# The cluster means of a fused convolution kernel, taken from the tiles in SBUF

## The chip, the cores and the metric

The kernel runs on one core of one Trainium2 chip. The metric is the device time of one execution in microseconds (us), as a median over several runs. A profiled execution is read beside it; its rows give the busy times, the waits and the order of the work. TensorE is called PE in those rows, its weight loads PEld, VectorE DVE, ScalarE ACT, GpSimd POOL and SyncE SP; a "q" behind an engine means its DMA issues.

## The reference, cut to what matters

The input `x` has 8 batches of 512 channels of 128 x 128. The first layer (L0) halves it with a grouped convolution, finds 8 clusters among the 256 channels of batch 0 alone, and takes the mean of each cluster's channels in every batch. A mixture model is fitted to those means, and what it gives scales the image in the rest of the layer. The second layer (L1) is a filtered resampling with a leaky slope.

```python
x = conv(sx, w_down, strides=(2, 2), padding=1, groups=256)    # (8, 256, 64, 64), 3x3, 2 inputs each
xx = x[0].reshape(256, 4096)                                     # batch 0 alone
labels = _kmeans_labels((xx - mn) / (mx - mn))                   # 10 rounds, 8 clusters
...                                                              # slabel: labels sorted by spread
soh = one_hot(slabel, 8)
v5 = einsum('bchw,ck->bkhw', x, soh / maximum(soh.sum(0), 1))   # the cluster means, all batches
mu, var = _gmm_fit(v5)                                           # 10 rounds, 2 components
...                                                              # gate from mu and var
out = L1(_bilinear_up_x2(up(gate * x + x)) + sx)
```

So the means of all batches need the labels, the labels need the convolution of batch 0 alone, and the mixture needs all means.

## The kernel before, in words

The program is five blocks, one behind another, with a barrier of all engines between them.

`convolution()` (line 133 on) goes through 64 units, 8 for each batch. A unit is 128 of the 256 channels (`cb`, two of them, `CB`) and 16 of the 64 output rows (`q`, four quarters, `NQ`). SP loads a unit's input rows into one of two buffers `rows_in` (line 186, about 4.2 MB), once DVE and PE have done the unit that used the buffer (`v_done`, `t_done`). DVE makes the first 9 of the 16 rows with one TENSOR_SCALAR (line 231) and 17 SCALAR_TENSOR_TENSOR (line 235), each waiting for the one before. PE makes the other 7 with 18 matmuls against diagonal weights (line 256); each fp32 matmul is two instructions in the trace, so a unit is 36. ACT copies PE's 7 rows from PSUM into the unit's tile `conv` (line 275) and stores the whole tile of 128 x 1024 to DRAM, `conv_dram` (line 281). The 8 units of batch 0 are written out; those of batches 1 to 7 are the body of a loop, so there are six jumps back. Within a batch the order is four quarters of `cb` 0, then four of `cb` 1 (`cb, q = n // NQ, n % NQ`). Units with `q == 0` are a little shorter on DVE, for they lack the row above.

`clusters(soh, sohn)` loads batch 0 back from `conv_dram` (`xx`), runs the k-means, and leaves the sorted labels as `soh` and their normalised form as `sohn`, 128 x 2 x 8.

`cluster_means(sohn)` (line 536 on) loads each batch back from `conv_dram` (`xb`, 4 MB, line 558), multiplies it on PE by `sohn` in pieces of 512 columns (line 569: 8 pieces of two channel blocks for each batch, outputs on 8 PSUM partitions), copies each piece on ACT (line 581), and stores the means to `mean_dram` (line 583).

`mixture(soh)` starts by loading `mean_dram` (line 650). `resample()` is the second layer with the end of the first; it reads `conv_dram` and `x` again and writes the output. Neither is touched.

The order on each engine is the order in which the code is written; no scheduler moves anything.

Of the kernel before, what the change touches and what calls it, by code (L numbers as in the profile page):

```python
# [13 lines left out]
P = 128  # L14
# [14 lines left out]
QR = 16  # L29
# [59 lines left out]
def build(nc, x, w_down, w_conv, w_up, bias, up_filter, down_filter, consts, out):  # L89
    at = constants()[1]  # L90
    ctx = ExitStack()
    with ctx:
# [40 lines left out]
        def convolution():  # L133
            with ExitStack() as own:
# [7 lines left out]
                tap_w = sb("tap_w", [P, CB, TAPS])  # L142
                diag = sb("diag", [P, CB * TAPS, P])
# [9 lines left out]
                UB = CB * NQ  # L153

                order = [(i, kh, kw) for i in range(2) for kh in (1, 0, 2) for kw in (1, 0, 2)]

                def conv_in(n, i, kh, kw, r0, r1):

                    c0 = (1, 0, 1)[kw]
                    return rows_in[n % 2][:, i, 2 * r0 + kh:2 * (r1 - 1) + kh + 1:2, c0:c0 + 2 * (63 if kw == 0 else 64) - 1:2]  # L160
# [4 lines left out]
                def _(sp):  # L165
# [11 lines left out]
                    def load(b, n, wait):  # L177
                        cb, q = n // NQ, n % NQ
                        if wait is not None:

                            sp.wait_ge(v_done, wait)
                            sp.wait_ge(t_done, wait)
                        lo = 1 if q == 0 else 0
                        src = x[bass.ds(b, 1)] if not isinstance(b, int) else x[b:b + 1]
                        src = src.rearrange("o (b c i) h w -> (o b) c i h w", b=CB, i=2)[cb]
                        sp.dma_start(rows_in[n % 2][:, :, lo:, :],
                                     src[:, :, 2 * QR * q - 1 + lo:2 * QR * (q + 1), :]).then_inc(in_loaded[n % 2], 16)

                    for n in range(UB):
                        load(0, n, n - 1 if n >= 2 else None)  # L190
                    with sp.Fori(1, B) as b:
                        for n in range(UB):
                            load(b, n, UB * b + n - 1)

                @block.vector
                def _(v):
# [21 lines left out]
                    def unit(b, n, first):  # L218
                        cb, q = n // NQ, n % NQ
                        v.wait_ge(in_loaded[n % 2], 16 * (n // 2 + 1) if first else (16 * (UB // 2)) * b + 16 * (n // 2 + 1))  # L220
                        if not (first and n < 2):

                            v.wait_ge(conv_stored[n % 2], 16 * (n // 2) if first else (16 * (UB // 2)) * b + 16 * (n // 2))
                        for s, (i, kh, kw) in enumerate(order):
# [3 lines left out]
                            src = conv_in(n, i, kh, kw, r0, V_ROWS)  # L228
                            last = s == TAPS - 1
                            if s == 0:  # L230
                                ins = v.tensor_scalar(dst, src, w, None, ALU.mult)
                            else:

                                v.wait_ge(vec_step, (TAPS - 1) * n + s if first else (TAPS - 1) * UB * b + ((TAPS - 1) * n + s))
                                ins = v.scalar_tensor_tensor(out=dst, in0=src, scalar=w, in1=dst, op0=ALU.mult, op1=ALU.add)  # L235
                            ins.then_inc(v_done if last else vec_step, 1)

                    for n in range(UB):
                        unit(0, n, True)
                    with v.Fori(1, B) as b:  # L240
                        for n in range(UB):
                            unit(b, n, False)

                @block.tensor
                def _(pe):
                    pe.wait_ge(diag_ready, 1)

                    def unit(b, n, first):
                        cb = n // NQ
                        pe.wait_ge(in_loaded[n % 2], 16 * (n // 2 + 1) if first else (16 * (UB // 2)) * b + 16 * (n // 2 + 1))  # L250
                        if not (first and n < 2):

                            pe.wait_ge(t_copied, n - 1 if first else UB * b + (n - 1))
                        acc = bank[n % 2][:, 0:T_ROWS * WO].rearrange("p (r w) -> p r w", r=T_ROWS)
                        for s, (i, kh, kw) in enumerate(order):
                            mm = pe.matmul(acc[:, :, (1 if kw == 0 else 0):],  # L256
                                           diag[:, cb * TAPS + (i * 3 + kh) * 3 + kw, :],
                                           conv_in(n, i, kh, kw, V_ROWS, QR), start=(s == 0), stop=(s == TAPS - 1),
                                           skip_group_check=True)
                        mm.then_inc(t_done, 1)  # L260

                    for n in range(UB):
                        unit(0, n, True)
                    with pe.Fori(1, B) as b:
                        for n in range(UB):
                            unit(b, n, False)

                @block.scalar
                def _(act):
                    def unit(b, n, first):  # L270
                        cb, q = n // NQ, n % NQ
                        act.wait_ge(t_done, n + 1 if first else UB * b + (n + 1))
                        if not (first and n < 2):
                            act.wait_ge(conv_stored[n % 2], 16 * (n // 2) if first else (16 * (UB // 2)) * b + 16 * (n // 2))
# [3 lines left out]
                        act.wait_ge(t_copied, n + 1 if first else UB * b + (n + 1))  # L278
                        act.wait_ge(v_done, n + 1 if first else UB * b + (n + 1))
                        rows = conv_dram[cb * P:(cb + 1) * P] if first else conv_dram[bass.ds(C * b + cb * P, P)]  # L280
# [3 lines left out]
                    for n in range(UB):  # L284
                        unit(0, n, True)
# [988 lines left out]
```

## Time and profile before

| | us |
|---|---|
| median of 3 runs (lowest to highest) | 7656.16 (7654.64 to 7658.82) |
| the profiled execution's own time | 7660.9 |
| its span, first to last instruction | 7658.7 |
| convolution, last group of 17 on DVE: begin, length | 1012.05, 14.43 |
| last issue of the convolution's stores | 1026.69 |
| first load of `cluster_means` issued | 1206.51 |
| first load of the mixture issued | 1336.74 |

Over the whole span PE is busy for 7119.1 us (93%), DVE for 5921.4 (77%), ACT for 4596.5 (60%) and POOL for 2518.8 (33%). These shares mix stages with different limits, and the resampling is by far the longest, so for a change in the first 1340 us the stages have to be read one by one. The page's 40 slices are 191 us each: the convolution is the first five and a bit, the clusters, the means and the mixture are the next three.

### The profile page before, as it was taken

What the parts mean: (1) busy time and instruction counts of PE and PEld (TensorE: products, weight loads), DVE (VectorE), ACT (ScalarE), POOL (GpSimd) and SP (SyncE); (2) the same over time, 40 slices, a digit from 0 to 9 for tenths busy, and PEclk for the clock granted to TensorE, in tenths of its full rate; (3) what the DMA queues carried; (4) which work ended last, traced back from release to release, by engine and by line L of the source; (5) the groups of instructions that cost most, each with busy time, mean ns of one, the idle gap of its engine ahead of it and who ended that gap; (6) DMA issues with size and microseconds to landing.
All of it is one profiled execution on the core that took longest, in us unless ns stands there. A gap on an engine that the chain in (4) does not pass through costs nothing.

```text
span 7658.7 us, 691127 instructions
## 1 busy us (share of the span) xinstructions
PE 7119.1 (93%) x302021; PEld 6407.7 (84%) x302021; DVE 5921.4 (77%) x11619; ACT 4596.5 (60%) x9070; POOL 2518.8 (33%) x3076
## 2 busy tenths in 40 slices
PE   7999967029999999999999999999999999999999
PEld 3444442029999999999999999999999999999998
DVE  8999950877777777777777777777777777777776
ACT  0000002337777777777777777777777777777776
POOL 0000000014444444444444444444444444444443
PEclk9999978569999999999999999999999999999999
DMA  7777724003333333333333333333333333333332
GB/s 303 316 310 308 310 118 183 3 24 96 96 96 96 96 96 96 96 96 96 96 96 96 96 96 96 96 96 96 96 96 95 96 96 96 96 96 96 96 96 80
DMA packets 1261531, 925.62 MB, mean 121 GB/s; under 512 B 183504, under 2 KB 1233104, under 8 KB 1242576
## 3 DMA queue, kind: packets, MB, share of 16 engines
q1 hardware_dynamic: 1252112, 890.13, 36.2%
q10 hardware_dynamic: 9344, 34.61, 1.7%
q8 instruction: 32, 0.52, 0.0%
q14 instruction: 43, 0.35, 0.0%
HBM read 621.50 MB, written 303.04 MB: 121 GB/s over the span
## 4 chain that ended last, share of the span: by engine, by line
PE 78%; issue 0%; DVE 0%; DMA 0%; ACT 0%; SPq 0%; POOL 0%; DVEq 0%
PE bank L1009 26%; PE bank L1004 24%; PE twin L1004 13%; PE twin L1009 13%; PE twin L1139 2%; DVE x_sum L1237 0%; DMA img<-in_x 0%; DVE leaky L1213 0%; DMA low<-conv_dram 0%; SPq L915 0%; ACT dn L1204 0%; ACT slope_t L1173 0%; POOL img L963 0%; DVE up L1222 0%; SPq L916 0%
## 5 line engine op out<-in xcount | busy, mean ns | idle before, releaser
L1213 DVE SCALAR_TENSOR_TENSOR leaky<-bank,slope_t 128x512 f32<-128x512 f32 x4096 | 2636.5, 685 | 1034.9 <-ACT slope_t L1173 1034.9
L1004 PE MATMUL bank<-up_t,up 64*64 64x133 f32 x65536 | 2760.3, 276 | 7.1 <-issue 6.3
L1009 PEld LDWEIGHTS bank<-down_t,leaky 64*64 64x64 f32 x131072 | 2235.9, 135 | 101.8 <-issue 92.9
L1009 PE MATMUL bank<-down_t,leaky 64*64 64x35 f32 (+1 forms) x131072 | 2306.3, 222 | 10.0 <-issue 8.0
L1173 ACT ACTIVATE slope_t<-bank 128x512 f32<-128x512 f32 x4096 | 2225.6, 599 | 7.9 <-PE bank L1004 7.9
L1004 PEld LDWEIGHTS bank<-up_t,up 64*64 64x64 f32 x65536 | 2041.1, 133 | 9.5 <-issue 9.5
L972 POOL TENSOR_TENSOR low_d<-low_v 128x252 f32<-128x252 f32 x512 | 310.9, 607 | 5038.9 <-ACT low_v L1195 5038.9
L1189 ACT ACTIVATE res<-twin 128x512 f32<-128x512 f32 x1024 | 611.6, 597 | 1447.7 <-PE twin L1009 1447.7
L1237 DVE SCALAR_TENSOR_TENSOR x_sum<-lift,coef,img 128x128 f32<-128x128 f32 x4096 | 1428.9, 409 | 11.7 <-POOL img L963 11.7
L1004 PE MATMUL twin<-up_t,x_sum 64*64 64x133 f32 x32768 | 1386.5, 278 | 9.2 <-DVE x_sum L1237 5.3
L1009 PE MATMUL twin<-down_t,dn 64*64 64x35 f32 (+1 forms) x65536 | 1358.8, 221 | 6.0 <-issue 5.7
L1009 PEld LDWEIGHTS twin<-down_t,dn 64*64 64x64 f32 x65536 | 1263.6, 135 | 6.8 <-issue 6.8
L1204 ACT ACTIVATE dn<-bank 128x512 f32<-128x512 f32 x2048 | 1135.5, 625 | 8.3 <-PE bank L1009 8.3
L963 POOL TENSOR_TENSOR img<-img,bias_all 128x512 f32<-128x512 f32 x1024 | 1041.7, 1036 | 7.5 <-DMA img<-in_x 7.3
L256 PE MATMUL twin<-rows_in,diag 128*128 128x448 f32 (+1 forms) x2304 | 929.5, 560 | 95.1 <-DMA rows_in<-in_x 91.4
L1004 PEld LDWEIGHTS twin<-up_t,x_sum 64*64 64x64 f32 x32768 | 1008.3, 133 | 10.8 <-issue 10.8
L1222 DVE COPY up<-twin 128x512 f32<-128x512 f32 x1024 | 708.6, 692 | 294.8 <-PE twin L1004 273.7
L256 PEld LDWEIGHTS twin<-rows_in,diag 128*128 128x128 f32 x2304 | 431.1, 189 | 592.8 <-issue 522.0
L235 DVE SCALAR_TENSOR_TENSOR conv<-rows_in,tap_w,conv 128x576 f32<-128x576 f32 (+3 forms) x1088 | 880.9, 810 | 45.3 <-issue 7.0
L1182 ACT ACTIVATE up<-twin 128x512 f32<-128x512 f32 x1024 | 611.6, 597 | 123.0 <-PE twin L1004 76.7
L275 ACT ACTIVATE conv<-twin 128x448 f32<-128x448 f32 x64 | 34.8, 544 | 988.3 <-PE twin L256 988.3
L978 POOL TENSOR_TENSOR lift<-low_f,low_v 128x504 f32<-128x504 f32 x512 | 565.5, 1105 | 40.1
(154 smaller groups left out, 2154.7 us busy)
## 6 DMA issues: line engine op xcount, KB each, us to landing
img<-in_x SPq DMA_DIRECT2D x1024, 256.0 KB, 2.9
out<-res SPq DMA_DIRECT2D x1024, 256.0 KB, 2.2
rows_in<-in_x SPq DMA_DIRECT2D x48, 4224.0 KB, 14.0
rows_in<-in_x SPq DMA_DIRECT2D x16, 4096.0 KB, 13.8
conv_dram<-conv ACTq DMA_DIRECT2D x64, 512.0 KB, 4.2
xb<-conv_dram SPq DMA_DIRECT2D x8, 4096.0 KB, 13.2
low<-conv_dram SPq DMA_DIRECT2D x1024, 32.0 KB, 2.2
xx<-conv_dram SPq DMA_DIRECT2D x2, 2048.0 KB, 10.3
```

Of the source, the lines that this page charges most:

```text
L235: ins = v.scalar_tensor_tensor(out=dst, in0=src, scalar=w, in1=dst, op0=ALU.mult, op1=ALU.add)
L256: mm = pe.matmul(acc[:, :, (1 if kw == 0 else 0):], diag[:, cb * TAPS + (i * 3 + kh) * 3 + kw, :], conv_in(n, i, kh, kw, V_ROWS, QR), star ...
L963: nc.gpsimd.tensor_tensor(pix, pix, bg[:, :, None].to_broadcast([P, 4, W]), ALU.add).then_inc(biased, 1)
L1004: return pe.matmul(acc[cols(c), a:b], src[cols(rt), cols(c)], up_t[cols(rt), a:b], start=first, stop=False, skip_group_check=True)
L1009: return pe.matmul(acc[cols(c), a:b], src[cols(rt)], down_t[cols(rt), k, a:b], start=first, stop=False, skip_group_check=True)
L1173: nc.scalar.activation(slope_t[e][i][:], u2_acc[e][i][:], ACT.Copy, scale=SLOPE * GAIN).then_inc(slope_out, 1)
L1182: nc.scalar.activation(up1[p][:, 0].rearrange("p e h -> p (e h)"), u1_acc[0], ACT.Copy).then_inc(u1_out0, 1)
L1189: nc.scalar.activation(res[1 - p][:].rearrange("p (e i) w -> p e (i w)", e=2), twin[:, :, 0:D2], ACT.Copy).then_inc(res_ready, 1)
L1204: nc.scalar.activation(dn1[p][:, e].rearrange("p j i h -> p (j i h)"), d1_acc[e][:], ACT.Copy).then_inc(d1_out, 1)
L1213: v.scalar_tensor_tensor(out=leaky[1 - m % 2][:, e, i].rearrange("p k w -> p (k w)"), in0=u2_acc[e][i][:], scalar=GAIN, in1=slope_t[e][i][ ...
L1222: v.tensor_copy(up1[m % 2][:, 1].rearrange("p e h -> p (e h)"), u1_acc[1]).then_inc(u1_out1, 1)
L1237: ins = v.scalar_tensor_tensor(out=x_sum[n % 2][:, e, i, :], in0=lift[n // 2][:, 2 * (n % 2) + e, :], scalar=cf, in1=img[n % 2][:, e, i, : ...
```

## The change

The convolution is split in two. `first_convolution()` does the 8 units of batch 0 alone. `clusters()` follows, and now keeps `xx` and the weights beyond its end; the normalised labels are written into `sohp`, 128 x 2 x 32, whose columns 8 to 31 are zero. `other_convolutions(sohp, xx)` then does the 56 units of batches 1 to 7 and makes the means on the way. `cluster_means()` is gone. Within a batch the units alternate between the channel blocks (`cb, q = n % CB, n // CB`), so that the two units of one quarter are neighbours.

A unit's means are four matmuls (line 341 of the changed kernel), for the four quarters of its 1024 columns: 128 x 32 weights, 256 columns each, and each writes 32 PSUM partitions of its own (`acc[32 * c:32 * (c + 1)]`). PE does unit n's taps first and then the means of unit n-1, when DVE's and ACT's parts of that tile are in (`v_done`, `t_copied`). The two units of a quarter add up in one PSUM bank (2 or 3, in turn). ACT copies that bank as 128 x 256 into `cm` and stores it with four DMAs (`store_means`). The tile of unit n-2 may only be written again when its means are made: DVE and ACT wait for `mean_mm` in addition to what they waited for. Batch 0's means are made from `xx` before PE's first taps of batch 1. Batch 1 is written out and batches 2 to 7 are a loop, so there are five jumps back.

Three places, as the engines' instructions stand. PE, in the written-out part, from the end of one unit to the begin of the one after (before: `twin` is the PSUM of the taps, `diag` the weights):

```order
L256 MATMUL twin<-rows_in,diag 128x7x63
L256 MATMUL twin<-rows_in,diag 128x448
L256 MATMUL twin<-rows_in,diag 128x448 [waits t_copied,in_loaded0]
L256 MATMUL twin<-rows_in,diag 128x7x63
L256 MATMUL twin<-rows_in,diag 128x448 x2
```

The same place in the changed kernel:

```order
L361 MATMUL twin<-rows_next,diag 128x7x63
L361 MATMUL twin<-rows_next,diag 128x448
L341 MATMUL bank<-conv_next,sohp 32x256 [waits mean_copied,next_t_copied,next_v_done]
L341 MATMUL bank<-conv_next,sohp 32x256 x3
L361 MATMUL twin<-rows_next,diag 128x448 [waits next_t_copied,next_loaded0]
L361 MATMUL twin<-rows_next,diag 128x7x63
```

Four matmuls have moved in between the last tap of a unit and the first of the next, and they wait for DVE and ACT. DVE, at the first instruction of a unit, before:

```order
L235 SCALAR_TENSOR_TENSOR conv<-rows_in,tap_w,conv 128x9x63 [waits vec_step]
L235 SCALAR_TENSOR_TENSOR conv<-rows_in,tap_w,conv 128x576 [waits vec_step]
L231 TENSOR_SCALAR conv<-rows_in,tap_w 128x576 [waits conv_stored1,in_loaded1]
L235 SCALAR_TENSOR_TENSOR conv<-rows_in,tap_w,conv 128x9x63 [waits vec_step]
L235 SCALAR_TENSOR_TENSOR conv<-rows_in,tap_w,conv 128x576 [waits vec_step] x2
```

and now, in the convolution of the other batches:

```order
L332 SCALAR_TENSOR_TENSOR conv_next<-rows_next,tap_w,conv_next 128x9x63 [waits next_step]
L332 SCALAR_TENSOR_TENSOR conv_next<-rows_next,tap_w,conv_next 128x576 [waits next_step]
L329 TENSOR_SCALAR conv_next<-rows_next,tap_w 128x576 [waits mean_mm,next_stored1,next_loaded1]
L332 SCALAR_TENSOR_TENSOR conv_next<-rows_next,tap_w,conv_next 128x9x63 [waits next_step]
L332 SCALAR_TENSOR_TENSOR conv_next<-rows_next,tap_w,conv_next 128x576 [waits next_step] x2
```

The unit's first instruction has one wait more, for PE. SP, from the clusters' loads to the mixture's, before:

```order
L362 DMA xx<-conv_dram 128x4096 x2
L294 UNCONDITIONAL_BRANCH
L553 UNCONDITIONAL_BRANCH [waits barrier_Pool_Activation_PE_DVE_SP_release]
L558 DMA xb<-conv_dram 128x2x4096 x2
L558 DMA xb<-conv_dram 128x2x4096 [waits cm_mm] x6
L537 UNCONDITIONAL_BRANCH
L647 UNCONDITIONAL_BRANCH [waits barrier_Pool_Activation_PE_DVE_SP_release]
L650 DMA data<-mean_dram 16x8x256 x8
```

and now, up to the first loop:

```order
L490 DMA xx<-conv_dram 128x4096 x2
L422 UNCONDITIONAL_BRANCH
L304 UNCONDITIONAL_BRANCH [waits barrier_Pool_Activation_PE_DVE_SP_release]
L147 DMA rows_next<-in_x 128x2x4096 x2
L147 DMA rows_next<-in_x 128x2x4224 [waits next_t_done,next_v_done] x6
L296 UNCONDITIONAL_BRANCH
```

The eight loads `xb` are gone, and the first loads of batch 1 stand behind the clusters' barrier. Behind the last unit, ACT has one copy of 128 x 256 (line 386) and four stores of means (line 392) ahead of the barrier before the mixture. The diff, cut to its core:

```diff
-        def convolution():
+        def load_rows(sp, rows_in, in_loaded, b, n):
+            cb, q = n % CB, n // CB
...
+        def first_convolution():
...
-                    for n in range(UB):
-                        load(0, n, n - 1 if n >= 2 else None)
-                    with sp.Fori(1, B) as b:
-                        for n in range(UB):
-                            load(b, n, UB * b + n - 1)
+                    for n in range(UB):
+                        if n >= 2:
+                            sp.wait_ge(v_done, n - 1)
+                            sp.wait_ge(t_done, n - 1)
+                        load_rows(sp, rows_in, in_loaded, 0, n)
...
+        def other_convolutions(sohp, xx):
...
+                def cnt(b, n, per=1, of=1):
+                    return (UB // of * per) * b + ((n // of) - UB // of) * per
+                def batches(eng, unit):
+                    for n in range(UB):
+                        unit(1, n)
+                    with eng.Fori(2, B) as b:
+                        for n in range(UB):
+                            unit(b, n)
...
+                @block.vector
+                def _(v):
+                    def unit(b, n):
+                        cb, q = n % CB, n // CB
+                        v.wait_ge(in_loaded[n % 2], cnt(b, n + 2, per=16, of=2))
+                        if ahead(b, n, 2):
+                            v.wait_ge(conv_stored[n % 2], cnt(b, n, per=16, of=2))
+                            v.wait_ge(mean_mm, cnt(b, n + UB - 1))
...
+                @block.tensor
+                def _(pe):
+                    def means(acc, tile, cb):
+                        for c in range(4):
+                            mm = pe.matmul(acc[32 * c:32 * (c + 1), 0:256], sohp[:, cb, :], tile[:, 256 * c:256 * (c + 1)],
+                                           start=(cb == 0), stop=(cb == CB - 1), skip_group_check=True)
+                        mm.then_inc(mean_mm, 1)
+                    def means_of(b, n):
+                        pe.wait_ge(v_done, cnt(b, n + 1))
+                        pe.wait_ge(t_copied, cnt(b, n + 1))
+                        if n % CB == 0:
+                            pe.wait_ge(mean_copied, cnt(b, n, of=2) + (NQ - 1))
+                        means(bank[2 + n // CB % 2], conv[n % 2][:].rearrange("p r w -> p (r w)"), n % CB)
+                    def unit(b, n):
...
+                        mm.then_inc(t_done, 1)
+                        if n > 0:
+                            means_of(b, n - 1)
+                        elif ahead(b, n, 1):
+                            means_of(b - 1, UB - 1)
+                    for g in range(NQ):
+                        if g >= 2:
+                            pe.wait_ge(mean_copied, g - 1)
+                        for cb in range(CB):
+                            means(bank[2 + g % 2], xx[:, cb, QR * WO * g:QR * WO * (g + 1)], cb)
+                    batches(pe, unit)
+                    means_of(B - 1, UB - 1)
...
+                    def store_means(b, q):
+                        act.wait_ge(mean_mm, cnt(b, 2 * q + 2 + UB))
+                        if not (isinstance(b, int) and NQ * b + q < 2):
+                            act.wait_ge(cm_stored[q % 2], cnt(b, 2 * q + UB, per=4 * 16, of=4))
+                        nc.scalar.activation(cm[q % 2][:], bank[2 + q % 2][:, 0:256], ACT.Copy).then_inc(mean_copied, 1)
+                        act.wait_ge(mean_copied, cnt(b, 2 * q + 2 + UB, of=2))
...
+                        for c in range(4):
+                            at = QR * WO * q + 256 * c
+                            act.dma_start(dst[:, at:at + 256], cm[q % 2][32 * c:32 * c + K]).then_inc(cm_stored[q % 2], 16)
...
-        def cluster_means(sohn):
...
-        convolution()
-        clusters(soh, sohn)
-        cluster_means(sohn)
+            first_convolution()
+            xx = own.enter_context(nc.sbuf_tensor("xx", [P, CB, PX], F32))
+            clusters(soh, sohp, xx)
+            other_convolutions(sohp, xx)
```

## Rows read from the trace of the kernel before

**Rows 1.** The page, part 4: chain that ended last, shares by engine.

```profile
PE 78%; issue 0%; DVE 0%; DMA 0%; ACT 0%; SPq 0%; POOL 0%; DVEq 0%
```

**Rows 2.** Windows: length, busy of PE, PEld, DVE, ACT, POOL; clock, DMA, GB/s.

```profile
160.00:1027.00 867.00, 810.92 (x2014) 375.66 (x2012) 811.97 (x1009) 30.47 (x56) 0.00 (x0) 0.99 0.77 307
1027.00:1206.50 179.50, 96.82 (x406) 76.93 (x406) 55.36 (x182) 17.04 (x26) 0.00 (x0) 0.66 0.07 27
1206.50:1336.70 130.20, 112.58 (x256) 23.09 (x256) 0.00 (x0) 37.57 (x64) 0.00 (x0) 0.93 0.68 266
1690.00:7659.00 5969.00, 5942.82 (x298406) 5848.57 (x298405) 4633.09 (x9178) 4395.90 (x8683) 2499.44 (x3049) 1.00 0.33 95
```

**Rows 3.** Timeline of DVE, convolution: start us, length us, instruction, idle before.

```profile
531.71 0.81 DVE L231 TENSOR_SCALAR conv<-rows_in,tap_w 128x576 f32<-128x576 f32 x1 [2.29 <-issue]
...
536.97 10.77 DVE L235 SCALAR_TENSOR_TENSOR conv<-rows_in,tap_w,conv 128x512 f32<-128x512 f32 x13 [1.18 <-issue]
547.65 0.81 DVE L231 TENSOR_SCALAR conv<-rows_in,tap_w 128x576 f32<-128x576 f32 x1
...
562.85 0.80 DVE L231 TENSOR_SCALAR conv<-rows_in,tap_w 128x576 f32<-128x576 f32 x1
...
593.23 0.81 DVE L231 TENSOR_SCALAR conv<-rows_in,tap_w 128x576 f32<-128x576 f32 x1
...
608.01 0.81 DVE L231 TENSOR_SCALAR conv<-rows_in,tap_w 128x576 f32<-128x576 f32 x1
...
656.03 0.81 DVE L231 TENSOR_SCALAR conv<-rows_in,tap_w 128x576 f32<-128x576 f32 x1 [2.38 <-issue]
```

**Rows 4.** Waits, convolution's window: us in total, times, longest.

```profile
DVE conv L231 <- issue: 14.0, 6, 2.4
DVE conv L235 <- issue: 7.0, 6, 1.2
```

**Rows 5.** Timeline of PE, convolution: two units.

```profile
592.49 14.42 PE L256 MATMUL twin<-rows_in,diag 128*128 128x448 f32 x36 [0.39 <-DMA rows_in<-in_x]
607.51 14.43 PE L256 MATMUL twin<-rows_in,diag 128*128 128x448 f32 x36 [0.60 <-DMA rows_in<-in_x]
```

**Rows 6.** Timeline of ACT, convolution: the copies behind those units.

```profile
592.13 0.54 ACT L275 ACTIVATE conv<-twin 128x448 f32<-128x448 f32 x1 [13.54 <-PE twin L256]
...
607.02 0.54 ACT L275 ACTIVATE conv<-twin 128x448 f32<-128x448 f32 x1 [14.35 <-PE twin L256]
```

**Rows 7.** Source L186, the loads of rows_in.

```profile
DMA to landing us min/median/max: 13.4/14.0/33.9
```

**Rows 8.** Timeline of ACT, start of the kernel: the first unit's copy.

```profile
54.71 0.55 ACT L275 ACTIVATE conv<-twin 128x448 f32<-128x448 f32 x1 [52.68 <-PE twin L256]
```

**Rows 9.** Timeline of PE, start of the kernel: the first units.

```profile
37.73 31.10 PE L256 MATMUL twin<-rows_in,diag 128*128 128x448 f32 x72 [37.73 <-DMA rows_in<-in_x]
```

**Rows 10.** Timeline, cluster_means: its first loads.

```profile
1206.51 29.48 SPq L558 DMA_DIRECT2D xb<-conv_dram  x3
```

**Rows 11.** Timeline of PE, cluster_means: from the first landing on.

```profile
1219.31 5.98 PE L569 MATMUL twin<-xb,sohn 128*8 128x512 f32 x8 [13.94 <-DMA xb<-conv_dram]
1225.13 3.60 PE L569 MATMUL bank<-xb,sohn 128*8 128x512 f32 x8
```

**Rows 12.** Timeline, end of cluster_means and start of the mixture.

```profile
1332.57 0.27 ACTq L583 DMA_DIRECT2D mean_dram<-cm  x1
1336.74 3.65 SPq L650 DMA_DIRECT2D data<-mean_dram  x8
```

**Rows 13.** Lines by form, cluster_means: busy us, mean ns, idle before.

```profile
L569 PE MATMUL bank<-xb,sohn 128*8 128x512 f32 x124 | 55.8, 592 | 0.0
...
L569 PEld LDWEIGHTS bank<-xb,sohn 128*8 128x8 f32 x125 | 11.2, 90 | 42.4 <-issue 42.4
```

**Rows 14.** Timeline of PE, resampling: two groups of 64x64 matmuls.

```profile
3001.58 0.66 PE L1004 MATMUL bank<-up_t,up 64*64 64x133 f32 x16
3002.04 0.66 PE L1004 MATMUL twin<-up_t,x_sum 64*64 64x133 f32 x16
```

More of the change, by code:

```diff
@@ L152, in convolution @@
                 t_copied = sem("t_copied")
[L153 to L160, printed above, removed]
                 block = own.enter_context(nc.Block())
@@ L216, in _ @@
                             n += 1
[L218 to L223, printed above, removed]
+                    for n in range(UB):
+                        cb, q = n % CB, n // CB
+                        v.wait_ge(in_loaded[n % 2], 16 * (n // 2 + 1))
+                        if n >= 2:
+                            v.wait_ge(conv_stored[n % 2], 16 * (n // 2))
                         for s, (i, kh, kw) in enumerate(order):
@@ L246, in _ @@
                     pe.wait_ge(diag_ready, 1)
[L248 to L253, printed above, removed]
+                    for n in range(UB):
+                        cb = n % CB
+                        pe.wait_ge(in_loaded[n % 2], 16 * (n // 2 + 1))
+                        if n >= 2:
+                            pe.wait_ge(t_copied, n - 1)
                         acc = bank[n % 2][:, 0:T_ROWS * WO].rearrange("p (r w) -> p r w", r=T_ROWS)
@@ L264, in _ @@
-                    with pe.Fori(1, B) as b:
-                        for n in range(UB):
-                            unit(b, n, False)
                 @block.scalar
                 def _(act):
[L270 to L274, printed above, removed]
+                    for n in range(UB):
+                        cb, q = n % CB, n // CB
+                        act.wait_ge(t_done, n + 1)
+                        if n >= 2:
+                            act.wait_ge(conv_stored[n % 2], 16 * (n // 2))
@@ L281, in unit @@
                         act.dma_start(rows[:, q * QR * WO:(q + 1) * QR * WO],
                                       conv[n % 2][:].rearrange("p r w -> p (r w)")).then_inc(conv_stored[n % 2], 16)
-                    for n in range(UB):
-                        unit(0, n, True)
-                    with act.Fori(1, B) as b:
-                        for n in range(UB):
-                            unit(b, n, False)
+                        if n % CB == 0 and n > 0:
+                            store_means(b, n // CB - 1)
+                        elif n == 0 and ahead(b, n, 1):
+                            store_means(b - 1, NQ - 1)
@@ L289, in _, with clusters @@
+                    for g in range(NQ):
+                        store_means(0, g)
+                    batches(act, unit)
+                    store_means(B - 1, NQ - 1)
                     for i in range(2):
-                        act.wait_ge(conv_stored[i], 16 * B * UB // 2)
-        def clusters(soh, sohn):
+                        act.wait_ge(conv_stored[i], 16 * (B - 1) * UB // 2)
+                        act.wait_ge(cm_stored[i], 4 * 16 * B * NQ // 2)
+        def clusters(soh, sohp, xx):
```

169 lines of the change are left out of this document (96 added, 73 removed).

## The prediction

> **What bounds the kernel now.** I read the chain of waits first. It is PE for 78% [rows 1], and the reader should distrust that for this change: the chain names the resampling, which the change does not touch. So I read the windows by stage next [rows 2]. They show four stages with four different limits. In the resampling PE is busy for 5942.82 of 5969 us. In the convolution DVE (811.97 of 867) and PE (810.92) are both nearly full, with the DMA engines at 0.77. In `clusters` nothing is full: it is a chain of small steps. In `cluster_means` PE is busy for 112.58 of 130.20 us and DVE does nothing at all. That stage is what goes, and the question is what its work costs where it now lies: beside a convolution in which DVE sets the pace and PE has hardly any room.
>
> Then I read the timelines of the convolution. A unit takes DVE 15.20 us (547.65 to 562.85), and 14.78 if it lacks a row (593.23 to 608.01) [rows 3]. PE needs 14.42 for its 36 instructions [rows 5]. DVE waits for nothing there but at each jump back: twice for "issue", together 21.0 us over six jumps, 3.5 each [rows 4]; a batch of eight units is 124.32 (531.71 to 656.03) [rows 3]. PE begins a unit when its load lands: the load is issued when DVE ends a unit, at 593.23, and PE's next unit begins at 607.51 [rows 3, 5], 14.28 later, of which the transfer is 14.0 [rows 7]. ACT begins its copy at 607.02 [rows 6], so PE is done 0.99 us before DVE ends the same unit at 608.01 [rows 3]. This 0.99 (1.10 for the unit before, from 592.13 to 593.23) is the room into which the new work must go, because DVE now also waits for PE's means.
>
> **What is removed.** The order shows that all of `cluster_means` goes, its loads included. From its first load to the mixture's first load is 1336.74 - 1206.51 = 130.23 us [rows 10, 12]. All of it lay on the path, for the barriers let nothing lie beside it. The DMA traffic of these loads goes too, but no other transfer ran beside it that would gain.
>
> **What is added on the path.**
>
> The second pipeline has to fill. Its first load is 4 MB, like `xb`'s, which landed 12.80 us after its issue (1206.51 to 1219.31) [rows 10, 11]. I take +12.8. The bounds are 12 and 15: two loads are issued together in both cases.
>
> The second pipeline has to start. In the first one PE begins at 37.73 and its first copy comes at 54.71 [rows 8, 9], 16.98 us, against 14.53 in the middle (592.49 to 607.02) [rows 5, 6]: 2.4 late. The third load waits for that, so DVE's third unit begins 16.98 + 14.3 = 31.3 after the first, where two short units need 2 x 14.78 = 29.6: +1.7. The means of the first unit lie in front of it now, another 0.6. I take +2.3; bounds 1 and 5.
>
> Batch 0's means (32 matmuls of 256 columns from `xx`) stand ahead of PE's first taps. By the serial price below they would last 8 x 1.7 = 14 us, some 17 with the slow begin that [rows 11] show (5.98 us for the first 8 instructions, 3.60 for the next); by the concurrent price 4 to 7. The cover is the 12.8 us of the first load. I take 0; up to 5 if serial.
>
> The tail. Behind the last unit PE makes the last means (about 0.8 with its wait), ACT copies 256 columns (448 columns take 0.54 [rows 6]; I take 0.4 and 0.2 for two wakes), issues four stores (0.27 for one [rows 12], I take 0.3 each, 1.2), and from the last issue to the mixture's first load it is 4.17 (1332.57 to 1336.74) [rows 12]. Sum 6.8; bounds 6 and 8. The first convolution's own tail is the one that stood there before. The store of a tile, ahead of that, is covered.
>
> Jumps back: five where there were six: -3.5 [rows 4]. Zeroing `sohp` is one small DVE instruction in the time of `xx`'s load: 0. The other order of units changes nothing in their number or size; in batch 0 it costs the gain of one short unit, 0.1.
>
> Sum so far: -130.2 + 12.8 + 2.3 + 6.8 - 3.5 = -111.8.
>
> **What is added beside other work: the price of the means.** A unit adds four matmuls, eight instructions of 256 columns, to PE. The nearest row by operation is `cluster_means`: a group of 8 instructions of 512 columns lasts 3.60 us [rows 11] and one instruction 0.592 [rows 13], so one begins every (3.60 - 0.59) / 7 = 0.43 us, 0.84 ns a column, and drains for 0.16 behind that. At that rate the means of a unit are 2048 columns x 0.84 = 1.7 us. The nearest row by shape is the resampling: 16 instructions of 133 columns on 64 x 64 pieces of the array begin every 0.46 us (3001.58 to 3002.04) [rows 14], 0.216 ns a column, 3.9 times faster, because four pieces work at once. The change writes four separate groups of 32 output partitions, the same device with other cuts; at that rate a unit's means are 0.44 us. No row here shows pieces of 128 x 32. I take the concurrent price, since the form that the change writes is the form that [rows 14] show working, and keep 1.7 as the other end.
>
> Around them PE changes from whole-array to cut-up matmuls and back. I add a drain of 0.16 on one side (the other is in the 14.42) and two weight loads that nothing hides: 0.09 for 8 columns [rows 13], I take 0.1 and 0.15. So PE's unit becomes 14.42 + 0.44 + 0.16 + 0.25 = 15.3 us, between 15.0 and 15.5.
>
> [...]
>
> Is 15.3 too much? A batch of eight takes PE 122.4 us, and DVE with its jump back 124.3 [rows 3]: PE has caught up at each jump. Within a batch it falls back by 0.1 a unit against 15.2, and 0.5 in each of the two short ones, against a room of 1.0 less the 0.75 that the means themselves take. So DVE waits a few tenths in some units and the jumps' 3.5 us take most of it in: 0.3 a batch, +2 us in all, bounds 0 and 8. Queued behind DVE's new wait is only its own next unit, and behind that SP's load after next; ACT's new waits are for means that PE made a unit earlier, and its four store issues (about 2 us a quarter) fall into 14 us of idle time [rows 6]. The stores of 32 KB in all a quarter are nothing beside 4 MB a unit.
>
> **Sum.** -111.8 + 2 = -110 us. The profiled execution's own time was 7660.9, 2.2 above its span and 4.7 above the median 7656.16; against its own time that is 7551, against the median 7546. I forecast 7546.
>
> **Rivals.**
>
> *Serial means.* The four column groups do not overlap. For it: it is what PE did with `sohn` [rows 11]. Against it: [rows 14]. PE's unit is 14.42 + 1.72 + 0.4 = 16.5, a batch 132 against 124.3, +7.7, seven times 54 us, and 5 at the start: 7546 - 2 + 59 = 7603.
>
> *Half concurrent.* Two pieces at a time: 0.86, a unit 15.7, a batch 126, +1.7 to 3, so 12 to 20 us: 7556 to 7565.
>
> *Slower than before.* Each of the eight instructions waits for the one before to drain and for its own weights: 0.21 + 0.16 + 0.15 = 0.52, a unit's means 4.2 us, PE's unit 18.8, a batch 150 against 124.3, +26, times seven 182: 7546 - 2 + 182 = 7726. It decides once a batch has lost 110 / 7 = 15.7 us, that is from 17.5 us a unit, or means of 3.1 us. In [rows 11] weight loads were hidden and instructions overlapped their drains, which speaks against it.
>
> [...]
>
> **How the numbers follow.** The forecast case (7538 to 7554) has 0.64; half concurrent and the stall at the jumps together 0.17; serial 0.13; slower 0.03; the rest, 0.03, is a loss of most of the gain by something unseen. 7546 is the likeliest. The range must take in the half concurrent case, whose price is unknown from the rows, and the serial one, which is a bound of the unknown cost: 7536 to 7604. A measurement of this kernel cannot tell less than 0.2%, 15 us, from no change. Faster by more than that are all cases but the slower one and part of the rest: 0.95; within it 0.01; slower 0.04.
>
> **What would show it.** Right: the rows of line 341 on four column groups begin nearly together and a unit's eight span about 0.6 us; DVE's units stay at 15.2 us; the second convolution's first DVE instruction comes 13 us after its load's issue; from the first convolution's end to that issue it is 180 us as before; the last DVE instruction of the convolution comes near 1218 us and the mixture's first load near 1225 instead of 1336.74. [...] The time itself fails me if the means cost over 1.1 us a unit.

## The result, and the profile after

The changed kernel takes 7526.72 us (median of four runs, 7524.66 to 7528.54), the kernel before 7655.40 in the same comparison (7654.10 to 7658.82): 128.7 us less, a ratio of 0.9831 with a 95% interval of 0.9814 to 0.9848. The forecast was 7546, with a range from 7536 to 7604. The direction and the build of the sum held, but the kernel gained 19 us more, and the time lies below the range.

The profiled execution has a span of 7522.9 us and shows where. I read it in the order of the forecast's sum. First DVE in the second convolution, and SP's first load ahead of it: start, length, what, idle time before and its releaser.

```profile
338.51 44.71 SPq L147 DMA_DIRECT2D rows_next<-in_x  x4
338.56 5.57 PE L341 MATMUL bank<-xx,sohp 128*32 128x256 f32 x64 [1.18 <-PEq L422]
...
352.14 0.81 DVE L329 TENSOR_SCALAR conv_next<-rows_next,tap_w 128x576 f32<-128x576 f32 x1 [14.11 <-DMA rows_next<-in_x]
352.16 30.44 PE L361 MATMUL twin<-rows_next,diag 128*128 128x448 f32 x72 [8.03 <-DMA rows_next<-in_x]
```

The fill is 352.14 - 338.51 = 13.6 us (forecast 12.8), and PE makes batch 0's means in 5.57 of them, so that they cost nothing. Next PE across two unit borders in the loop, to be held against [rows 5]:

```profile
716.13 0.64 PE L341 MATMUL bank<-conv_next,sohp 128*32 128x256 f32 x8
716.70 14.43 PE L361 MATMUL twin<-rows_next,diag 128*128 128x448 f32 x36
731.05 0.64 PE L341 MATMUL bank<-conv_next,sohp 128*32 128x256 f32 x8
731.62 14.43 PE L361 MATMUL twin<-rows_next,diag 128*128 128x448 f32 x36
```

A unit's means move PE's next tap by 0.57 us (716.13 to 716.70), and PE's whole unit is 14.92 (716.70 to 731.62), less than DVE's 15.19. The concurrent price was right. Now DVE over a jump back of the loop, which lies between the group that begins at 703.26 and the unit that begins at 717.60; this answers to [rows 3]:

```profile
703.26 14.43 DVE L332 SCALAR_TENSOR_TENSOR conv_next<-rows_next,tap_w,conv_next 128x567 f32<-128x567 f32 x17
717.60 0.81 DVE L329 TENSOR_SCALAR conv_next<-rows_next,tap_w 128x576 f32<-128x576 f32 x1
718.44 14.03 DVE L332 SCALAR_TENSOR_TENSOR conv_next<-rows_next,tap_w,conv_next 128x567 f32<-128x567 f32 x17
732.39 0.81 DVE L329 TENSOR_SCALAR conv_next<-rows_next,tap_w 128x576 f32<-128x576 f32 x1
```

There is no idle time. Before, the same spot had 2.29 us and 1.18 us of "issue" [rows 3], 21.0 us over six jumps [rows 4]; I had expected the 3.5 us at each of the five jumps that are left. The waits of the two DVE lines say the same for the whole convolution (us in total, times, longest); the "issue" lines of [rows 4] are gone:

```profile
DVE conv_next L329 <- DMA rows_next<-in_x: 15.4, 4, 14.1
...
DVE conv_next L329 <- PE bank L341: 1.8, 2, 1.5
```

Part 3 of the page holds a trace of the cause that I had not read. It lists the packets that carry instructions. First the kernel before, then the changed one:

```profile
q14 instruction: 43, 0.35, 0.0%
```

```profile
q14 instruction: 15, 0.12, 0.0%
```

Last the end of the convolution, against [rows 12]:

```profile
1200.89 0.64 PE L341 MATMUL bank<-conv_next,sohp 128*32 128x256 f32 x8 [1.17 <-DVE conv_next L332]
1201.05 0.36 ACTq L405 DMA_DIRECT2D conv_dram<-conv_next  x1
1201.64 0.38 ACT L386 ACTIVATE cm<-bank 128x256 f32<-128x256 f32 x1 [1.91 <-PE bank L341]
1202.06 1.33 ACTq L392 DMA_DIRECT2D mean_dram<-cm  x4
1204.98 1.29 SPq L728 DMA_DIRECT2D data<-mean_dram  x3
```

DVE ends the convolution at 1200.84; the mixture's first load is issued at 1204.98, 131.8 us earlier than the 1336.74 of before. From there to the end the two profiled executions differ by 4.1 us more (6322.0 and 6317.9), in stages that the change does not touch; in the profile of `after_again`, the changed kernel once more, that part was 6320.4, so I count it as scatter.

### The profile page after: what moved, and what is told of

Read it like the earlier page. It is cut to its first block, busy times and chain, and to the rows that moved or that the text cites. A ratio compares the mean times of both kernels' runs of the same rounds, so it can differ in the third digit from the quotient of the medians.

```text
span 7522.9 us, 691936 instructions
## 1 busy us (share of the span) xinstructions
PE 7038.6 (94%) x302277; PEld 6399.7 (85%) x302277; DVE 5921.7 (79%) x11620; ACT 4569.9 (61%) x9038; POOL 2523.5 (34%) x3076
## 4 chain that ended last, share of the span: by engine, by line
PE 79%; issue 0%; DVE 0%; DMA 0%; ACT 0%; SPq 0%; POOL 0%; DVEq 0%
PE bank L1087 26%; PE bank L1082 25%; PE twin L1082 13%; PE twin L1087 13%; PE twin L1217 2%; DVE x_sum L1315 0%; DMA img<-in_x 0%; DVE leaky L1291 0%; DMA low<-conv_dram 0%; SPq L993 0%; POOL img L1041 0%; SPq L994 0%; DVE up L1300 0%; ACT dn L1282 0%; ACT res L1267 0%
## 5 line engine op out<-in xcount | busy, mean ns | idle before, releaser
L361 PE MATMUL twin<-rows_next,diag 128*128 128x448 f32 (+1 forms) x2016 | 809.6, 559 | 16.9 <-DMA rows_next<-in_x 16.3
L332 DVE SCALAR_TENSOR_TENSOR conv_next<-rows_next,tap_w,conv_next 128x576 f32<-128x576 f32 (+3 forms) x952 | 770.8, 810 | 33.7
L361 PEld LDWEIGHTS twin<-rows_next,diag 128*128 128x128 f32 x2016 | 375.2, 188 | 433.9 <-issue 399.8
L1053 POOL TENSOR_TENSOR low_f<-low_d,cst 128x504 f32<-128x504 f32 x512 | 571.3, 1116 | 0.0
```

The source lines that it names most:

```text
L361: mm = pe.matmul(acc[:, :, (1 if kw == 0 else 0):], diag[:, cb * TAPS + (i * 3 + kh) * 3 + kw, :], conv_in(rows_in, n, i, kh, kw, V_ROWS, ...
```

## The experiments

**Where the jumps' stalls went.** The trace has the time and the size of every packet of q14, 8192 bytes each, and they can be set beside DVE's instructions. Counted in the traces, with register and branch instructions, DVE runs 294 instructions in one round of the convolution's loop before, and 299 after the change, so the loop did not get shorter. In the loop before, q14 fetches five packets a round, near DVE's instructions 1, 12, 23, 144 and 276 (at 529.69, 535.16, 540.41, 591.75 and 645.29 us; 29 packets from 280 to 1010 us). Where code runs for the first time, the packets come 123 and 132 of DVE's instructions apart in the kernel before (at 167.19, 218.21 and 273.08 us, with one more at 221.72) and 136, 134 and 123 in the changed one (52.39 to 176.58 us, 414.23 to 497.37, and from there to 548.59). So I take 128 instructions for a fetched block. From that I placed boundaries between fetched blocks near instructions 12, 140 and 268: the loop lies over four blocks. In the changed kernel, by the fetches of the loop's first round at 497.37 and 548.59 us, they are near 56 and 184: three blocks, and after the first round q14 fetches nothing until the convolution is over (the next packet comes at 1206.62). The blocks and their boundaries are an estimate of mine, worked out from where the packets come, give or take 4 instructions; no row shows them. Two more packets come in that first round, at 521 and 526 us. They come at about the same time, 521 to 530 us, in all four padded versions of the changed kernel, so they are counted as no boundary. Theory A: a loop over three blocks by this count is not fetched again, one over four is fetched again each round, and DVE waits for that. (Where an expectation says that a loop stays in the engine's store, a trace can show this much of it: that no packet comes in its later rounds.) By this theory it depends on where the code happens to stand, not on what was changed. The rivals were B, that the jump or the traffic of that moment costs the time, and C, that the new order of units carries the pipeline over it.

The first run moves the kernel before, and nothing else:

```diff
+        filler = sb("filler", [P, 84])
                     v.memset(ones[:], 1.0).then_inc(ready, 1)
+                    for i in range(84):
+                        v.memset(filler[:, i:i + 1], 0.0)
```

> The kernel before with 84 one-column memsets on DVE ahead of its first wait, inside the 19 us in which it idles for the first loads. Nothing else changes. Theory A (fetch): the 3.5 us at each jump back in the convolution are instruction fetches on DVE; the loop of 294 instructions lies over four fetched blocks of 8 KB and does not stay in the engine's store; moved by 84 instructions it lies over three, like the changed kernel's, and stays. Then all six stalls go: 7655 - 21 = 7634 us, and the instruction queue q14 has about 15 packets where it had 43. Theory B (load): the stalls belong to the jump itself or to what the DMA queues carry at that time: 7655, stalls as before. Theory C (order of units): as B here.

Measured: 7635.89 us against 7659.98 (ratio 0.9969, 0.9959 to 0.9980), 24 us less. The page's row and DVE over the first jump back (the loop's second round begins at 278.82):

```profile
q14 instruction: 14, 0.11, 0.0%
```

```profile
269.58 9.32 DVE L238 SCALAR_TENSOR_TENSOR conv<-rows_in,tap_w,conv 128x567 f32<-128x567 f32 x11
278.82 0.81 DVE L234 TENSOR_SCALAR conv<-rows_in,tap_w 128x576 f32<-128x576 f32 x1
279.66 14.03 DVE L238 SCALAR_TENSOR_TENSOR conv<-rows_in,tap_w,conv 128x567 f32<-128x567 f32 x17
```

All six stalls are gone, 14 packets came where there had been 43, with none between 232.74 and 1007.57 us, and no work was taken out: 84 instructions were added. Theory B has fallen. The rows had 21.0 us of stalls and the kernel gained 24; where the other 3 us come from no row says.

The second run puts 44 memsets at the same place of the changed kernel:

> The changed kernel with 44 one-column memsets on DVE ahead of its first wait, which puts its convolution loop over four blocks as the kernel before has it. Theory A (fetch): five jumps back stall for 3.5 us each, 7527 + 17.5 = 7544 us, and the packets of q14 rise from 15 by about 25. Theories B and C: 7527, no stall.

Measured: 7559.34 us (7553.75 to 7565.55), 28 us above the 7531.52 that the control beside it took. Here DVE at a jump back, and the page's row:

```profile
600.19 0.81 DVE L332 TENSOR_SCALAR conv_next<-rows_next,tap_w 128x576 f32<-128x576 f32 x1 [2.56 <-issue]
601.03 1.66 DVE L335 SCALAR_TENSOR_TENSOR conv_next<-rows_next,tap_w,conv_next 128x567 f32<-128x567 f32 x2
605.23 12.33 DVE L335 SCALAR_TENSOR_TENSOR conv_next<-rows_next,tap_w,conv_next 128x512 f32<-128x512 f32 x15 [2.53 <-issue]
```

```profile
q14 instruction: 40, 0.33, 0.0%
```

The direction is A's, the size is larger: 5.1 us a jump, 25.7 in all, and 5.6 us of waits for PE where the changed kernel has 1.8:

```profile
DVE conv_next L335 <- issue: 13.4, 5, 3.2
DVE conv_next L332 <- issue: 12.3, 5, 2.6
DVE conv_next L332 <- PE bank L344: 5.6, 4, 2.2
```

The times of the packets, set beside DVE's rows, tie both stalls to a packet. In the kernel before, at the jump of [rows 3], DVE falls idle at 529.42; a packet begins at 529.69, the next at 535.16, and DVE goes on at 531.71 and 536.97. In `after_pad44` it is idle from 597.63, the packets begin at 597.92 and 603.40, and it goes on at 600.19 and 605.23. In all eleven jumps of the two kernels DVE goes on 2.0 to 2.3 us after the first packet began and 1.8 to 1.9 us after the second, and the second begins 5.4 to 5.8 us after the first. What differs is the work that DVE does between the two stalls: five instructions (4.1 us) before, three (2.5 us) here. So the second stall is 1.2 us there and 2.5 here.

The control has 100 memsets, more than the slow version:

> Control: the changed kernel with 100 such memsets, more than in the run with 44, but a place over three blocks again by the count of instructions. Theory A: 7527 us within 3, no stall at the jumps. If the memsets themselves or any shift cost time, it is slower than the one with 44.

Measured: 7531.52 us (7526.76 to 7533.33), 15 packets on q14, no wait of DVE for "issue" in the convolution. So neither the memsets nor a shift as such bring the stalls.

Two kernels at the edge of the block count, with 6 and 22 memsets, two executions each:

> The changed kernel with 6 one-column memsets on DVE ahead of its loop. By the spots of the fetches its loop of 299 instructions begins about 56 instructions ahead of a boundary between fetched blocks of 128 instructions (uncertain by 4). Moved by 6 it is 50, and 50 + 256 = 306 still covers the 299: three blocks, no stall, 7527 to 7532. Rival (any shift may bring the stalls): unknown, up to 7560.

Measured: 7527.44 us, 15 packets on q14, no wait of DVE for "issue" in the convolution.

> The same with 22 memsets: 34 instructions ahead of the boundary, 34 + 256 = 290 is less than 299, so the loop's last instructions lie in a fourth block: the stalls come back at all five jumps, 7550 to 7560, with about 40 packets on q14. If it stays at 7530 the count of blocks is not what decides.

Measured: 7542.01 us and 40 packets. Six more instructions leave the 15 packets as they are, sixteen more bring 40, as the count has it. The size was less than I expected, for only one stall came with a jump:

```profile
DVE conv_next L332 <- issue: 12.1, 5, 2.6
```

```profile
599.96 0.81 DVE L332 TENSOR_SCALAR conv_next<-rows_next,tap_w 128x576 f32<-128x576 f32 x1 [2.44 <-issue]
600.80 14.04 DVE L335 SCALAR_TENSOR_TENSOR conv_next<-rows_next,tap_w,conv_next 128x567 f32<-128x567 f32 x17
```

5 x 2.4 = 12.1 us of the 15. The second packet comes here too, at 603.17, 5.35 us after the first at 597.82, but DVE works through: by the count the boundary now lies 34 instructions into the loop, near the end of the first group of 17, which lasts 14.04 us. How many blocks are refetched and how much of it DVE feels are two questions: `after_pad22` and `after_pad44` both have 40 packets, and stall for 2.4 and 5.1 us a jump. With 2.5 us of work ahead of the second spot the stall there was 2.5 to 3.2 us (`after_pad44`, five jumps), with 4.1 us it was 1.1 to 1.2 (before, six jumps), and here there was none.

Theory C had a run of its own, the order of units alone:

```diff
-                        cb, q = n // NQ, n % NQ
+                        cb, q = n % CB, n // CB
```

> The kernel before with the changed kernel's order of units alone: within a batch the two channel blocks alternate. Theory C (order of units): the two short units now stand together at the jump and let the pipeline run over it, so the stalls go, 7634 us. Theories A and B: the number of DVE instructions and their place are the same, 7655 us within 3, 21 us of stalls stay.

Measured: 7660.18 us against 7659.98 (ratio 1.0002, 0.9992 to 1.0011), with the stalls as they were, so C has fallen too:

```profile
DVE conv L231 <- issue: 13.5, 6, 2.3
DVE conv L235 <- issue: 6.7, 6, 1.2
```

**What the split costs.** The next kernel splits the convolution, but makes no means in it; `cluster_means` stands behind it for all batches.

```diff
                         mm.then_inc(t_done, 1)
-                        if n > 0:
-                            means_of(b, n - 1)
-                        elif ahead(b, n, 1):
-                            means_of(b - 1, UB - 1)
...
             other_convolutions(sohp, xx)
+            cluster_means(sohp)
```

> The changed kernel with its split convolution and its order of units, but the means are not made in the convolution: cluster_means stands behind it as before, for all eight batches. It is the split alone. Theory: against the kernel before it pays a second fill of the pipeline (13.6 us), a second start (1.6) and a second drain of stores (about 4), and gains the 21 us of fetch stalls at the jumps back, since its loop stays over three fetched blocks. Sum -2: the time of before within 4 us, 7654 to 7660. Rival (the forecast's term of 3.5 us for the jumps): 14 to 18 us above before, 7672. Its units on DVE tell what the means cost beside the convolution: 15.19 and 14.79 us with no waits for PE if the means cost nothing there.

Measured: 7656.73 us against 7661.59 (ratio 0.9993, 0.9984 to 1.0003), 5 us less with an interval that includes no change. The split's own costs and the 21 us of stalls that went nearly cancel; with my term of 3.5 us it would have been 14 to 18 us slower. So without the luck of the place, the split would have had to be paid out of the 130 us.

**What the means cost beside the taps.** The first run takes the concurrency away: all four matmuls write the same 32 partitions, in two banks.

```diff
-mm = pe.matmul(acc[32 * c:32 * (c + 1), 0:256], sohp[:, cb, :], ...
+mm = pe.matmul(acc[c // 2][0:32, 256 * (c % 2):256 * (c % 2 + 1)], sohp[:, cb, :], ...
```

> The changed kernel with all four matmuls of a unit's means on the same 32 output partitions, in two PSUM banks of 512 columns; ACT makes two copies of 32 x 512 where it made one of 128 x 256. It takes the concurrency away. Theory: the eight instructions follow one another at 0.21 us, 1.7 us a unit; PE's unit is 14.4 + 1.7 + 0.15 = 16.2 us, a batch 130 us where DVE needs 120.7, so seven times 9 and 4 at the start: 7527 + 68 = 7595 us. Rival: PE's room swallows most of it because the loads let PE run ahead: under 7560.

Measured: 7592.89 us (median of four, ratio 0.9912, 0.9895 to 0.9928), 66 above the changed kernel in the comparison of the result. The mixture's first load comes at 1265.97, 61.0 us later than in the changed kernel. (The profiled execution took 7617.08; the part behind that load is 31 us longer than in the changed kernel's profile, where nothing was changed, and I leave it out.) PE over two unit borders, and what DVE waited for:

```profile
723.53 1.91 PE L341 MATMUL bank<-conv_next,sohp 128*32 128x256 f32 x8
725.37 14.43 PE L361 MATMUL twin<-rows_next,diag 128*128 128x448 f32 x36
739.73 1.91 PE L341 MATMUL bank<-conv_next,sohp 128*32 128x256 f32 x8
741.58 14.43 PE L361 MATMUL twin<-rows_next,diag 128*128 128x448 f32 x36
```

```profile
DVE conv_next L329 <- PE bank L341: 58.2, 54, 4.4
```

The means now move the next tap by 1.84 us, PE's unit is 16.21, and DVE waits for PE in 54 of 56 units. This is the serial rival, built: the means cost the 1.7 us that the forecast gave them, PE's unit is 0.3 shorter than its 16.5, and the time lies 10 below its 7603.

The second run issues the means twice, the second time into a bank that nobody reads:

> The changed kernel with each unit's four means matmuls issued a second time into a PSUM bank that nobody reads. Theory (PE sets the pace once its own unit is longer than DVE's): 14.93 + 0.45 to 0.57 = 15.4 to 15.5 us a unit against 15.09 on the mean of a batch, 123.5 a batch against 120.7: seven times 2.8 less the room, 15 to 22 us: 7545. Rival (the room of 1 us in each unit is what counts, and 0.5 fits in): 7527 to 7531.

Measured: 7542.11 us (7541.19 to 7542.55), 15 above the changed kernel in the comparison of the result; by the mixture's first load (1218.01 against 1204.98) it is 13. The rows give the price of four matmuls on four column groups by itself:

```profile
720.98 0.64 PE L341 MATMUL bank<-conv_next,sohp 128*32 128x256 f32 x8
721.43 0.61 PE L344 MATMUL bank<-conv_next,sohp 128*32 128x256 f32 x8
721.98 14.43 PE L364 MATMUL twin<-rows_next,diag 128*128 128x448 f32 x36
...
737.34 8.14 PE L364 MATMUL twin<-rows_next,diag 128*128 128x448 f32 x20
```

The second set begins 0.45 us after the first. PE's unit is 15.36 us (721.98 to 737.34), 0.17 over DVE's. So what counts in the end is PE's pace, not only the room in one unit, and 13 to 15 us lies at or just under the low end of the first theory's range.

**A version that goes further.** The fill of 13.6 us is time in which DVE has nothing to do. This kernel issues batch 1's first two loads during the clusters, once the Gram matrix is done, into buffers that `xs` and `xs_t` no longer need.

```diff
+                xs = flat[0].rearrange("p (b x) -> p b x", b=CB)         # in rows_next[0]
+                xs_t = flat[1].rearrange("p (t c) -> p t c", t=NB)      # in rows_next[1]
...
+                    sp.wait_ge(gram_mm, CB)
+                    for n in range(2):
+                        load_rows(sp, rows_next, next_loaded, 1, n)
```

> The changed kernel with batch 1's first two loads issued during the clusters, once the Gram matrix is done, into buffers that take the place of xs and xs_t. It takes the fill of the second pipeline away. Theory: the fill of 13.6 us goes; batch 0's means on PE (5.6 us), which it hid, then stand ahead of PE's first taps and delay the third unit by about 4: 7527 - 9 = 7518 us. Rival: the transfers slow the clusters' chain or the start is bound by PE altogether: no gain.

Measured: 7521.20 us (7519.59 to 7523.31; ratio 0.9820, 0.9804 to 0.9836). DVE now begins beside batch 0's means, and PE's first taps come behind them (rows from the second profile of this version, `early_again`):

```profile
339.00 0.81 DVE L327 TENSOR_SCALAR conv_next<-rows_next,tap_w 128x576 f32<-128x576 f32 x1 [0.53 <-PEq L420]
339.01 6.26 PE L339 MATMUL bank<-xx,sohp 128*32 128x256 f32 x64 [1.18 <-PEq L420]
...
345.20 28.59 PE L359 MATMUL twin<-rows_next,diag 128*128 128x448 f32 x72
```

To size the difference, both kernels ran once more on one chip, in five rounds:

> The changed kernel itself once more, beside the version with early loads on the same chip, to size the difference between the two: 7527 to 7532 us.

> The version with batch 1's first two loads issued during the clusters, once more beside the changed kernel. From its first profile, in which the mixture's first load came 9.4 us earlier than in the changed kernel's: 9 us below the changed kernel of this call. Rival: the 9 us are the scatter between chips, and the two differ by under 3.

Measured: 7527.19 us (7525.88 to 7529.16) and 7518.96 us (7514.58 to 7520.48). The ranges do not touch; the early loads gain 8.2 us. The ratios to the kernel before are 0.9832 (0.9819 to 0.9846) and 0.9820 (0.9806 to 0.9833).

## Why the prediction was wrong, by its own steps

- *What is removed*, 130.2 us: `split_only` has it back in full, and with it nearly the time of before.
- *The fill*, +12.8: 13.6 measured. *The start*, +2.3: the third unit began 31.20 us after the first, where two short units need 29.58, so 1.6; 1.5 of it is DVE's one long wait for PE. *Batch 0's means*, 0: 5.57 us under a fill of 13.6. Right.
- *The tail*, +6.8: 4.14 (1200.84 to 1204.98), below its lower bound of 6. To the first store's issue it was 1.22 (forecast 1.4), and the four issues took 1.33 (forecast 1.2). The term that was too large is the 4.17 us from the last issue to the next stage, taken from [rows 12]: here it is 1.9 (1203.07 to 1204.98). That store was 128 KB and these are 8 KB each; whether the size makes the difference no run shows.
- *The price of the means*: PE's unit 14.92, forecast 15.3, just below the range of 15.0 to 15.5. The concurrent 0.44 was right (0.43 to 0.45). Within a unit the taps' instructions begin every 0.394 us, 14.18 for 36, so both changes of shape together, weight loads included, cost 14.92 - 14.18 - 0.43 = 0.31: the first instruction of the means comes 0.48 behind the last tap, the next tap 0.31 behind the last of the means (0.22 is their own pace), and the second tap 0.50 behind the first. The 14.42 of [rows 5] already holds such a slow first tap (0.50) and the end of the last one, so the means added 0.50 to it, and of the 0.41 for drain and weight loads only some 0.06 was still to be added. That PE drains at the change of shape was an assumption of mine, which no row shows: with the weight loads it can weigh 0.31 us a unit here at most, and no row separates the two. *Beside other work*, +2: DVE's 56 units took 848.7 us (352.14 to 1200.84), and seven batches of 120.72 with the 1.6 of the start are 846.7: 2.0 more. The number is right, and that is luck: I had DVE wait for PE a few tenths in some units, because PE's unit was to be longer than DVE's. Behind the start DVE waited for PE for 0.3 us in all; the largest wait, 0.9 us, was for a load, and `split_only`, which makes no means, has one of 0.7 at the same spot.
- *Jumps back*, -3.5: **this is the step that failed.** It was -21.0. The rest of the sum was off by little: 0.8 - 0.7 - 2.7, and 1.6 us at the begin and in the clusters, which came out a little shorter. With -21 in place of -3.5 the forecast is 7528.5. A stall of PE's own at a jump back, for which the chances leave room, no run shows: in `one_group`, where PE sets the pace, its steps from taps to means and back are 0.48 and 0.31 us at every unit from 594 to 1228 us.

The failed step took a stall of the kernel before as a property of the jump, "3.5 each [rows 4]", and scaled it with the number of jumps. The trace had "issue" as the releaser, which says that the engine waited for nothing that the profile shows; I took its size and did not ask for its cause. The runs tie it to the instruction packets of q14: in all eleven jumps of the kernel before and of `after_pad44` the first stall ends 2.0 to 2.3 us after a packet began and the second 1.8 to 1.9 us after the next, and in the versions in which no packet comes at the jumps there is no stall. Whether they come depends on where the loop lies: moving a loop by 84 instructions took them away (`before_pad84`, 14 packets for 43, no stall for 21.0 us), by 44 brought them (`after_pad44`, 40 packets for 15, 25.7 us), by 100 did not (`after_pad100`, 15 packets, no stall). That it is the number of fetched blocks that decides is my count, and the eight kernels in the last section agree with it. The change moved the loop by accident, since it put other code ahead of it and other instructions into it (299 for 294).

The range failed with it. A stall without a known cause in a loop that the change rewrites is an unknown cost with two ends, and the good end, no stall at all, was 17.5 us below. I bounded the cost of the new work from both sides, and this one from neither.

What the change does by itself is best read between the two kernels that have no such stalls, run on the same chip: 7635.89 (`before_pad84`) and 7531.52 (`after_pad100`), 104 us apart. The other 24 us went with the stalls, and the kernel before could have been rid of them without the change.

## What to carry to other kernels

Work that a later stage does on data that it must load again is best done where the data still lies in SBUF, if the engine that takes it has room in each unit: compare that engine's whole unit, new work included, with the pacing engine's, as 14.92 against 15.19 here. When "issue" stands as the releaser at a loop's jump back, look at the instruction packets on the page and compare them with the number of rounds; if they grow with the rounds (here 43 with six jumps back, 14 without the stalls), try a shift by some tens of instructions before anything else (84 here, which gained 24 us). Before crediting a rewritten loop with a gain or a loss, see whether its stalls at the jump came or went.

## What the runs showed of the hardware that I had not expected

- Instruction packets on q14 are 8192 bytes each (43 of them are the page's 0.35 MB), and where code ran for the first time they came 123 to 136 of DVE's instructions apart, by my estimate one for about 128. A loop of 294 or 299 instructions was fetched again in each round where by the count it lies over four such blocks, and not where it lies over three: 43, 43 and 40, 40 packets (before, `before_order`, `after_pad44`, `after_pad22`) against 14, 15, 15, 15 (`before_pad84`, `after`, `after_pad100`, `after_pad6`). The refetch cost 2.4 us (`after_pad22`), 3.5 us (before) or 5.1 us (`after_pad44`) a round. The cost differs with the work that stands between the jump and the next boundary, as the second stall shows: 2.5 to 3.2 us behind 2.5 us of work, 1.1 to 1.2 behind 4.1. How much of its code DVE can hold, the runs do not tell.
- Four fp32 matmuls of 256 columns with 32 output partitions each are eight instructions. On one column group one begins every 0.216 us, 1.73 for the eight (`one_group`). On four groups four begin within 0.02 us and the next four 0.22 behind them, 0.43 to 0.45 for the eight (`after`, `means_twice`): about 4 times faster, for whole contractions of 128 rows. The forecast had 3.9 times, from the 64 x 64 pieces of [rows 14].
- Changing from whole-array to column-tiled matmuls and back cost PE 0.31 us a unit for both ways, weight loads included (14.92 - 14.18 - 0.43).
